# Layer-norm variances one token to a partition, inverses spread by TensorE, part sums moved between engines, modulation parts reordered

## The reference

```python
mod = (silu(c) @ wmod).reshape(2, 6, 1, 1024)            # c: (2, 1024), wmod: (1024, 6144)
sa, ca, ga, sb, cb, gb = mod[:, 0] ... mod[:, 5]
ga, gb = sign(ga) * max(|ga|, 0.25), sign(gb) * max(|gb|, 0.25)
h = layernorm(x) * (1 + ca) + sa                          # x: (2, 2048, 1024), over the 1024 features
q = h.transpose(2, 0, 1)                                  # (1024 features, batch 2, 2048 tokens)
prob = softmax(q @ q.T / sqrt(2048))                      # one 2x2 table for each feature
x = x + ga * (h + (prob @ q).transpose(1, 2, 0))
h = layernorm(x) * (1 + cb) + sb
x = x + gb * ((silu(h @ W_gate.T) * (h @ W_up.T)) @ W_down.T)   # 1024 -> 2752 -> 1024
```

## Time and profile before

| | us |
|---|---|
| median of 3 runs (2817.76 to 2823.97) | 2818.89 |
| profiled execution, its time | 2821.63 |
| profiled execution, its span | 2819.8 |
| TensorE busy | 2750.6 (98%) |
| VectorE busy | 1545.2 (55%) |
| ScalarE busy | 1059.7 (38%) |
| GpSimd busy | 156.1 (6%) |

### The profile page before, as it was taken

One profiled execution on the slowest core, in us unless ns is written; L12 is line 12 of the kernel. 1 busy time (PEld: TensorE's weight loads), 2 busy tenths in 40 slices (PEclk: granted clock), 3 DMA queues, 4 the chain that ended last, 5 costly groups with the idle time before them and its releaser, 6 DMA issues.

```text
span 2819.8 us, 32541 instructions
## 1 busy us (share of the span) xinstructions
PE 2750.6 (98%) x11784; PEld 2157.2 (77%) x11784; DVE 1545.2 (55%) x2057; ACT 1059.7 (38%) x1616; POOL 156.1 (6%) x206
## 2 busy tenths in 40 slices
PE   8988999998999999999999899999999999999999
PEld 3336887786888886788887788887788888888887
DVE  6988777764455534455443433335446446446544
ACT  4656455553243432334423211112343333333332
POOL 5200011000010000000100000000000000000000
PEclk9999999999999999999999999999999999999999
DMA  8675999989788879888879999999757657657654
GB/s 343 241 288 195 334 329 325 334 301 342 267 300 304 305 256 299 287 309 301 294 271 283 348 358 344 352 348 320 252 212 256 227 210 250 233 211 245 245 202 165
DMA packets 359711, 795.77 MB, mean 282 GB/s; under 512 B 25760, under 2 KB 154016, under 8 KB 350848
## 3 DMA queue, kind: packets, MB, share of 16 engines
q1 hardware_dynamic: 341648, 721.32, 73.3%
q0 software_dynamic: 17088, 59.78, 6.2%
q10 hardware_dynamic: 816, 12.58, 1.1%
HBM read 553.26 MB, written 240.32 MB: 281 GB/s over the span
## 4 chain that ended last, share of the span: by engine, by line
PE 86%; DMA 3%; issue 1%; SPq 1%; ACT 1%; DVE 1%; DVEq 0%; ACTq 0%
PE ps L1588 19%; PE ps L1589 19%; PE ps L1590 19%; PE ps L1651 10%; PE ps L1652 10%; PE ps L1653 10%; DMA x_raw_P<-xr_dram 1%; DMA h_dram<-ww 1%; DMA w_raw<-wdn 0%; SPq L397 0%; SPq L388 0%; DMA whl_dram<-w_lo_P 0%; PE ps L1598 0%; ACT x_raw_P L737 0%; PE ps L1599 0%
## 5 line engine op out<-in xcount | busy, mean ns | idle before, releaser
L1588 PE MATMUL ps<-x_hi_P,w_slot 128*128 128x512 f32 (+1 forms) x1848 | 724.5, 392 | 23.1 <-ACT vv L803 10.5
L1589 PE MATMUL ps<-x_lo_P,w_slot 128*128 128x512 f32 (+1 forms) x1848 | 723.2, 391 | 0.0
L1590 PE MATMUL ps<-x_hi_P,w_slot 128*128 128x512 f32 (+1 forms) x1848 | 722.9, 391 | 0.0
L1651 PE MATMUL ps<-hh,w_hi 128*128 128x512 f32 (+1 forms) x1232 | 481.1, 391 | 3.3 <-DVE w_lo L1354 2.0
L1652 PE MATMUL ps<-hl,w_hi 128*128 128x512 f32 (+1 forms) x1232 | 480.9, 390 | 0.0
L1653 PE MATMUL ps<-hh,w_lo 128*128 128x512 f32 (+1 forms) x1232 | 479.9, 389 | 0.0
L1588 PEld LDWEIGHTS ps<-x_hi_P,w_slot 128*128 128x128 f32 (+1 forms) x1848 | 344.4, 186 | 104.9 <-ACT vv L803 11.7
L1590 PEld LDWEIGHTS ps<-x_hi_P,w_slot 128*128 128x128 f32 (+1 forms) x1848 | 344.4, 186 | 78.3
L1589 PEld LDWEIGHTS ps<-x_lo_P,w_slot 128*128 128x128 f32 (+1 forms) x1848 | 344.5, 186 | 77.4
L1354 DVE TENSOR_TENSOR w_lo<-w_raw,w_hi 128x1408 fp32r<-128x1408 f32 x112 | 181.7, 1623 | 212.6 <-ACT w_hi L870 212.6
L1651 PEld LDWEIGHTS ps<-hh,w_hi 128*128 128x128 f32 (+1 forms) x1232 | 231.6, 188 | 53.3 <-DVE w_lo L1354 2.4
(11 more groups left out here) (181 smaller groups left out, 2651.6 us busy)
## 6 DMA issues: line engine op xcount, KB each, us to landing
w_slot<-whl_dram SPq DMA_DIRECT2D x420, 512.0 KB, 6.1
w_raw<-wds_dram SPq DMA_DIRECT2D x64, 704.0 KB, 4.6
hl_raw<-h_dram SPq DMA_DIRECT2D x56, 768.0 KB, 7.0
h_dram<-hb SPq DMA_DIRECT2D x30, 1280.0 KB, 9.8
whl_dram<-w_hi SPq DMA_DIRECT2D x140, 256.0 KB, 3.4
whl_dram<-w_lo_P SPq DMA_DIRECT2D x140, 256.0 KB, 4.2
w_raw<-wdn SPq DMA_DIRECT2D x48, 704.0 KB, 5.0
hl_raw<-h_dram SPq DMA_DIRECT2D x28, 1024.0 KB, 9.8
```

The lines of the kernel that those rows point to most:

```text
L1588: mm(bank, hi[:, w], x_hi[name][:, k, :], start=fresh and k == 0, stop=False, skip_group_check=not fresh)
L1589: mm(bank, hi[:, w], x_lo[name][:, k, :], start=False, stop=False, skip_group_check=not fresh)
L1590: ins = mm(bank, lo[:, w], x_hi[name][:, k, :], start=False, stop=k == KH - 1, skip_group_check=not fresh)
L1651: mm(bank, hi[0:n, w], hh[stage % 2][0:n, j, :], start=fresh and j == 0, stop=False, skip_group_check=not fresh)
```

## The change

Four things change, all in the opening.

1. **Variances with a token to a partition.** The squares become the stationary operand (128x128, four blocks of a chunk, `NTB` = 4) and one column of ones moves, so a chunk takes 16 matmuls with a result of 128x1 instead of 4 of 128x512. The variance of 512 tokens is then 128x4. `root` and `invert` work on 128x4. ScalarE builds four diagonal matrices from the inverses (`diagonal`, 4 instructions of 128x128), and TensorE multiplies all-ones weights with them (`spread`, one matmul of 128x512), which puts the inverse of each token on all partitions of a PSUM bank. `normalise` reads it there.
2. **Part sums.** In half 0 VectorE forms three of the four sums of four tiles (one instruction of 128x1024, one of 128x512 each), GpSimd one. In half 1 GpSimd forms all four, over six tiles each (5 additions), and TensorE takes two tiles directly.
3. **Order.** `parts` no longer interleave with `variances`; whole parts stand between them. `turn` of groups 0 and 1 comes ahead of all eight parts of group 2, where four of those came first. ScalarE's diagonal for chunk (1, 1) stands behind 14 of the 16 `square_sums` of u = 0.
4. **Transfers.** `save_xhat` goes out in two halves of 2 MB; a 64 KB identity matrix is loaded too.

```diff
-PRE = (4, 0)
+PRE = (4, 6)
+NTB = T // P
@@ gpsimd @@
                 if t == 0:
-                    sum_tiles(0, 0)
                     sum_tiles(0, 1)
-                    sum_tiles(1, 0)
-                    add_squares(0, 0)
-                    sum_tiles(1, 1)
                 else:
-                    add_squares(0, 0)
+                    for u, h in ((0, 0), (0, 1), (1, 0), (1, 1)):
+                        sum_tiles(u, h)
+                add_squares(0, 0)
@@ scalar @@
+                def diagonal(u, h):
+                    i = t * 4 + 2 * u + h
+                    act.wait_ge(inv_ready, i + 1)
+                    if i >= 2:
+                        act.wait_ge(rstd_ready, i - 1)
+                    for b in range(NTB):
+                        ins = s.activation(diag[:, h, b, :], eye_all[:], ACT.Identity, scale=inv[:, u, h, b:b + 1])
+                    ins.then_inc(diag_ready, 1)
...
                 root(1, 1)
-                square_sums(0, range(KD))
-                save_xhat(0)
-                square_sums(1, range(KD // 2))
+                square_sums(0, range(KD // 2))
+                save_xhat(0, 0)
+                square_sums(0, range(KD // 2, KD - 1))
+                diagonal(1, 1)
+                square_sums(0, range(KD - 1, KD))
+                save_xhat(0, 1)
                 if t:
                     copy_rows(0)
+                square_sums(1, range(KD // 2))
...
+                square_sums(1, range(KD // 2, KD - 2))
+                if t:
                     copy_rows(1)
-                square_sums(1, range(KD // 2, KD))
+                square_sums(1, range(KD - 2, KD))
@@ vector @@
+                def sum_tiles(u, h):
...
+                    v.tensor_tensor(two, xk[:, 0:2, :], xk[:, 2:4, :], ALU.add).then_inc(presum_chain, 1)
+                    dve.wait_ge(presum_chain, summed[0])
+                    v.tensor_tensor(presums[u][:, h, :], two[:, 0, :], two[:, 1, :], ALU.add).then_inc(presum_dve, 1)
                 def normalise(u, k):
-                        v.scalar_tensor_tensor(dbuf[u][:, :, k, b, :], dbuf[u][:, :, k, b, :], 1.0,
-                                               rstd[:, u, :, b * CC:(b + 1) * CC], ALU.mult, ALU.mult,
+                        v.scalar_tensor_tensor(dbuf[u][:, :, k, b, :], ps[:, RSTD_BANK[u]:RSTD_BANK[u] + 2, b * CC:(b + 1) * CC], 1.0,
+                                               dbuf[u][:, :, k, b, :], ALU.mult, ALU.mult,
...
-                    dve.wait_ge(rstd_ready, t * 4 + (2 * u + 4))
+                    dve.wait_ge(rstd_ready, t * 4 + (2 * u + 2))
@@ tensor @@
+                    if t and u == 1:
+                        pe.wait_ge(xhat_ready, 4 * KD)
+                    for k in range(PRE[t], KD):
+                        mm(ps_mean[u][h], ones[:], tok(xbuf[u][:, h])[:, k, :], start=k == PRE[t], stop=False)
...
-                        mm(ps_var[h], ones[:], sq_pair[:, j % 2, :], start=j == 0, stop=j == NSQ - 1).then_inc(sq_pair_used, 1)
+                        for b in range(NTB):
+                            ins = mm(ps_mean[u][h][:, b:b + 1], sq_pair[:, j % 2, b * P:(b + 1) * P], ones[:, 0:1],
+                                     start=j == b == 0, stop=j == NSQ - 1 and b == NTB - 1)
+                def spread(u, h):
+                    pe.wait_ge(diag_ready, t * 4 + (2 * u + h + 1))
+                    if t and u == 0:
+                        pe.wait_ge(xhat_ready, 2 * KD)
+                    mm(ps[:, RSTD_BANK[u] + h, :], ones[:], diag[:, h].rearrange("p b q -> p (b q)"), start=True, stop=True).then_inc(
+                        rstd_ready, 1)
+                means(0, 0)
+                means(0, 1)
                 if t == 0:
                     means(1, 0)
                     variances(0, 0)
                     means(1, 1)
                     variances(0, 1)
+                    spread(0, 0)
+                    variances(1, 0)
+                    spread(0, 1)
                     pe.wait_ge(silu_ready, 1)
-                    parts(0, range(2))
-                    variances(1, 0, 0, 2)
-                    variances(1, 1, 0, 3)
+                    parts(0, range(1))
+                    variances(1, 1)
+                    spread(1, 0)
+                    parts(0, range(1, 2))
+                    spread(1, 1)
+                    parts(0, range(2, 3))
                 else:
+                    parts(0, range(3, GROUP[0]))
                     means(1, 0)
                     means(1, 1)
+                    variances(0, 0)
+                    variances(0, 1)
+                    parts(1, range(1))
+                    spread(0, 0)
+                    spread(0, 1)
+                    variances(1, 0)
+                    parts(1, range(1, 2))
+                    spread(1, 0)
+                    variances(1, 1)
+                    parts(1, range(2, 3))
+                    spread(1, 1)
+                    parts(1, range(3, GROUP[1]))
-            parts(2, range(4))
             turn(0, ps_mod[0], ROWS[0] + ROWS[1], 0)
             turn(1, ps_mod[0], ROWS[0] + ROWS[1], ROWS[0])
-            parts(2, range(4, GROUP[2]))
+            parts(2, range(GROUP[2]))
```

More of the change, by code:

```diff
@@ L294, in bc, with tok2 @@
         return ap[:, None, :].broadcast_to([P, n, T])
+    def tok2(ap):
+        return ap.rearrange("p h k b c -> p h k (b c)")
     def tok(ap):
@@ L752, in _ @@
             root_f(1)
[L753 removed]
+            act.wait_ge(xh_stored[0], 64)
             for k in range(KH):
@@ L1487, in means @@
                     pe.wait_ge(x_loaded[u][h], t * 16 + 16)
-                    if t:
-                        pe.wait_ge(centred, 2 * (i + 1))
-                    for k in range(PRE[t], KD):
-                        ins = mm(ps_mean[u][h], ones[:], tok(xbuf[u][:, h])[:, k, :], start=k == PRE[t], stop=PRE[t] == 0 and k == KD - 1)
-                    if PRE[t]:
-                        pe.wait_ge(presum_ready, i + 1)
-                        ins = mm(ps_mean[u][h], ones[:], presums[u][:, h, :], start=False, stop=True)
@@ L1498, in variances @@
+                    mm(ps_mean[u][h], ones[:], presums[u][:, h, :], start=False, stop=True).then_inc(mean_mm, 1)
+                def variances(u, h):
                     i = 2 * u + h
-                    pe.wait_ge(std_ready, t * 4 + (i + 1))
+                    pe.wait_ge(centred, t * 8 + 2 * (i + 1))
                     for j in range(NSQ):
                         pe.wait_ge(sq_added, t * (4 * NSQ) + (i * NSQ + j + 3))
-                        mm(ps_var[h], ones[:], sq_pair[:, j % 2, :], start=j == 0, stop=j == NSQ - 1).then_inc(sq_pair_used, 1)
-                        if group is not None:
-                            modulate(group, part_of, range(2 * j, 2 * j + 2))
+                        for b in range(NTB):
+                            ins = mm(ps_mean[u][h][:, b:b + 1], sq_pair[:, j % 2, b * P:(b + 1) * P], ones[:, 0:1],
+                                     start=j == b == 0, stop=j == NSQ - 1 and b == NTB - 1)
+                        ins.then_inc(sq_pair_used, 1)
@@ L1506, in _ @@
+                def spread(u, h):
+                    pe.wait_ge(diag_ready, t * 4 + (2 * u + h + 1))
+                    if t and u == 0:
+                        pe.wait_ge(xhat_ready, 2 * KD)
[3 more added lines that the diff above has]
+                means(0, 1)
                 if t == 0:
-                    means(0, 0)
-                    means(0, 1)
```

100 lines of the change are left out of this document (58 added, 42 removed).

## The result

The changed kernel is slower. Its median is 2835.49 us (2832.74 to 2838.03, 6 runs), that of the kernel before in the same comparison 2819.69 us (2814.59 to 2824.74, 6 runs): ratio 1.0053, 95% interval 1.0041 to 1.0066, some 15 us. I had predicted 2827.9 with a range of 2813 to 2836, and slower with a chance of 0.56. The direction held and the time lies within the range, half a microsecond under its upper end. The size was short by two fifths: 9.0 us forecast, 15.8 by the medians, 14.9 by the ratio.

What follows compares the result with a forecast made beforehand. TensorE was taken to bound the opening up to mean_f(0): -2.4 us without the clock plus 11.4 for clock returns gave +9.0 on the median of 2818.89, so 2827.9 us, range 2813 to 2836.

Steps and rivals of the forecast that it cites:

- clock-free sum: Opening's TensorE and ScalarE order without a fallen clock: mean_f(0) ends at 179.6 us, 2.4 us earlier than before.
- The chain: Opening: TensorE's and ScalarE's order binds, eight parts follow the turn, and VectorE waits some 15 us for TensorE.
- The price of the small matmul: New variance matmuls: 0.117 us a record, taken from the turn; four blocks are 8 records, 0.94 us.
- The rival of cheaper ones: Clock holds and small matmuls cost half the turn's row: -5.6 us more, 2810.9 us; chance 0.13.
- the clock that holds: Rival: weight loads keep TensorE's clock at 1.00 and idle is too short; -2.4 us, 2816.5 us; chance 0.22.
- 6 x 1.9 = 11.4: Clock term: dense TensorE work returns at low clock six times on the opening's chain, 1.9 us each.
- this doubling: Variances' weight loads may double at the lower clock: 0.94 us more for about six groups; with cold parts +7.5.
- what follows hangs on it one to one: Behind mean_f(0): centre_f(0) starts on its release, and the opening's gain or loss is handed on in full.
- One of the signs: Profile sign of the forecast: the turn would stand between 145 and 156 us.
- The rival of the lock: GpSimd's additions lengthen half 0's cross products on VectorE: +6 to +10 on the -2.4, 2824 to 2827 us; chance 0.10.
- The rival of the later transfer: A wmod part is 3 to 6 us late behind a 2 MB store: 2831 to 2834 us; chance 0.10.

Runs made afterwards that it cites:

- four parts cut: Changed kernel with parts 4 to 7 of group 2 reduced to one matmul on ones each, their loads left out, result wrong: 2821.31 us, ratio 1.0006.
- the table: Lists the kernel before, the changed kernel and follow-up kernels, with mean_f(0) end and first feed-forward product from one profile each, and median; ratios 0.9987 to 1.0115.
- diagonal first: Changed kernel with ScalarE's diagonal (1, 1) straight behind its root, ahead of the square sums, in both halves: 2830.07 us, ratio 1.0031.
- three fillers: Kernel with all edits and rows copied earlier, plus three unused 128x384 matmuls behind each variance's first three groups: 2816.8 us, ratio 0.9992 to the kernel before.
- tiles direct: Changed kernel without GpSimd's sums of tiles in half 1; TensorE takes all eight tiles itself: 2849.18 us, ratio 1.0106.
- row variances: Changed kernel with variances again as one 128x512 matmul a group, root and inverse over 128x512, no diagonals or spreads: 2834.73 us, ratio 1.0053.
- five fillers: Changed kernel with five unused 128x384 fp32r matmuls behind each of the first three groups of every variance: 2835.01 us, ratio 1.0056.

## Why the prediction was right in direction and short in size

My sum had a part free of the clock and a part for it. Set item by item against the trace of the changed kernel (an end is read where the next record starts, that of `mean_f(0)` at its own end):

| step | clock-free sum | measured | more |
|---|---|---|---|
| mean (1, 1) of half 0 ends | 33.8 | 37.2 | 3.4 |
| fourth spread of half 0 ends | 66.1 | 74.2 | 8.1 |
| first two spreads of half 1 end | 105.4 | 119.9 | 14.5 |
| last variance of half 1 starts | 115.1 | 132.4 | 17.3 |
| fourth spread of half 1 ends | 132.1 | 149.2 | 17.1 |
| turn ends | 144.5 | 162.6 | 18.1 |
| mean_f(0) ends | 179.6 | 197.4 | 17.8 |

- **The chain was the right one**, link by link: the same instructions end each wait, the turn is followed by eight parts that run at full clock (27.79 us for 28.0), and VectorE waits 15.47 us where I wrote "some 15 us". That last number tests the order and not the times: VectorE's work hangs on the turn as the parts do, and both came some 18 us late.
- **The price of the small matmul was right** at full clock: 0.115 us a record for 0.117 from the turn. The rival of cheaper ones falls with it. So does the clock that holds: most variances began at 1.00, but the granted clock came down in those of both halves (0.56 in 28 to 32 us, 0.50 in 44 to 48 and 104 to 108).
- **The step that was mis-sized is "6 x 1.9 = 11.4"**, which measured 17.8. I charged only the dense work that comes back after a slow stretch. The variances themselves run at the lower level: 40 records in half 1 took 8.62 us, 4.0 more than at 0.115. At full clock a variance waits for GpSimd, which hides part of that: the two variances of half 1 took 12.2 us together for my 9.8, and that of chunk (1, 0) in half 0 6.7 for 4.9. And a part behind one lost more than 1.9: it took 6.18 and 6.52 us in half 1 against 3.5, 2.7 and 3.0 more. I had named this doubling, but put it into the range's upper end and not into the forecast. With 17.8 the sum is 15.4, and the prediction 2834.3. The 17.8 is one profile's; the run with four parts cut had 3 us less of it.
- **Behind mean_f(0)** I said that what follows hangs on it one to one. To the first product the loss grew from 15.4 to 18.0 us: the second pair of square matmuls took 6.35 us at the lower clock, where before the first pair had met it with 5.40. The median shows 15.8, so some 2 us were given back further on or lie in the scatter. Over the kernels of the table the time by the ratio follows the first product to within 3.0 us, but for two (diagonal first, three fillers) that are off by 6.3 and 5.3; their profiled executions took 2.7 and 3.8 us more than their medians.
- **One of the signs failed with the term:** the turn stood at 160.7 to 162.6 us and not between 145 and 156.
- **The rival of the lock** is small: `cross` took 874 ns in the mean over 32, 3.9 us in all over the 752 of the kernel before, and VectorE had slack there. **The rival of the later transfer** is half right: no part of `wmod` was late, but VectorE's `centre` waited 4.62 us for a store at 104.66, under cover of TensorE. The cover is thin: with the diagonal first it was 7.67 us.

Put together: part sums on GpSimd in half 1 are worth 15 us (tiles direct), the variance form is even in this order (row variances), the order of ScalarE's diagonal costs 6 us, and eight parts between turn and `mean_f(0)` cost 10 that can be saved by placing three of them in waits behind it. What the fallen clock costs is argued from the rows, not shown by a time: five fillers held the clock, and their own work and longer waits for the diagonals cost as much as it gave.

## What to carry to other kernels

When work is moved off one engine in a chain over several, work out the next engine's time for the same stretch at the clock that it will have, and charge the slow matmuls themselves as well as the dense ones behind them. A wait of one engine in front of a long ordered stretch of another is bought off most cheaply by moving what has no early user behind the one that has: here three parts were worth 10 us. And when a wait is taken away, look for the next at once: diagonal, store, copy and load each held 2 to 8 us behind one another, and the fixes of the diagonal and of the stores showed half of their value or none when made singly. Before a few microseconds between two profiles are put down to an edit, compare a stretch that the edit leaves alone: here it differed by 3.

## What the runs showed of the hardware

- TensorE's clock fell to 1.2 GHz in a run of matmuls with 128 columns of weights and one moving column, with pauses of only 0.57 and 0.18 us ahead of the fall, and stayed there while TensorE was busy without a gap. It also fell in an alternation of these with matmuls of 256 moving columns, and stayed at 0.50 through both. The Trainium skill (TensorE: Matmul & The Clock Gate, Part 1) ties the lower rate to an idle array; this trace has it at busy 4.00 of 4.00 us, and the measurement decides. In the run with five 384-column matmuls behind a group it stayed at 1.00 through the variances, in the run with three it fell to 0.50.
- `normalise` with its inverse in PSUM took 684 ns in the mean, with both operands in SBUF and the same GpSimd work in the kernel 898. The medians are alike (686 and 681 ns); the longest of 64 was 692 ns with the operand in PSUM and 1749 with both in SBUF. So only the SBUF form was lengthened. That GpSimd's additions beside it are the reason fits the `cross` of the earlier trace rows but was not tested by itself. I had expected no gain from it.
- The 2 MB stores and the 1 MB loads delayed each other. With a load held back until the stores had landed, the four stores of half 0 took 11.8 us in the median for 16.3. And issuing the last store 11 us later (154.10 for 142.90) moved a wait of TensorE from one part's load (2.04 us) to another's (3.31); issued another 8 us later, it made no load late.
